# Input order and port use at the start of a macaron block: x ahead of the weights, two rounds of roots, GpSimd scaling eight weight groups

## The reference

```
x = x + 0.5 * ffn(layernorm(x))
x = x + mixer(layernorm(x))          # in-projection, causal conv, state space scan, gate, RMS norm, out-projection
x = x + 0.5 * ffn(layernorm(x))      # the same ffn weights
ffn(v): v = fwht(v * SU_ug) / 64
        u = v @ W_up.T * (Wscale_up * 64);  g = v @ W_gate.T * (Wscale_gate * 64)
        h = fwht(silu(g) * u * SU_dp) / 64
        return h @ W_down.T * (Wscale_dp * 64)
```

## Time and profile before

| what | value |
|---|---|
| time before, median of 3 runs | 1652.19 us (1651.5 to 1653.33) |
| time of the profiled execution | 1654.4 us |
| span of the profiled execution | 1652.4 us |
| PE busy | 1621.7 us, 98% of the span |
| DVE busy | 1034.9 us, 63% |
| ACT busy | 626.4 us, 38% |
| POOL busy | 378.9 us, 23% |

### The profile page before, as it was taken

How to read it: one execution, slowest core, us unless ns; L and a number is a source line. 1 busy time by engine, 2 the same in 40 slices (tenths; PEclk the granted TensorE clock), 3 DMA queues, 4 the chain that set the end, 5 groups by cost and what they waited for, 6 DMA issues and landing times.

```text
span 1652.4 us, 25046 instructions
## 1 busy us (share of the span) xinstructions
PE 1621.7 (98%) x9672; PEld 1312.8 (79%) x9672; DVE 1034.9 (63%) x2022; ACT 626.4 (38%) x934; POOL 378.9 (23%) x298
## 2 busy tenths in 40 slices
PE   6999999989999999999999999999999999999999
PEld 3788888867888778888878888877888878888887
DVE  6444445766676877777786777777675684543333
ACT  4333434454333464333355334256333342122111
POOL 1656663012221212222122122121122121000000
PEclk9999999999999999999999999999999999999999
DMA  9746554745455454444535444445445537556763
GB/s 296 286 151 245 205 217 166 268 156 159 155 159 162 132 177 145 161 161 152 160 121 175 164 150 166 161 138 182 157 154 158 164 117 227 167 181 188 218 201 130
DMA packets 253427, 290.46 MB, mean 176 GB/s; under 512 B 14464, under 2 KB 211200, under 8 KB 244096
## 3 DMA queue, kind: packets, MB, share of 16 engines
q1 hardware_dynamic: 253312, 288.88, 53.4%
HBM read 238.51 MB, written 50.33 MB: 175 GB/s over the span
## 4 chain that ended last, share of the span: by engine, by line
PE 73%; DVE 3%; ACT 2%; issue 1%; DMA 0%; SPq 0%; ACTq 0%; DVEq 0%
PE bank L1185 30%; PE bank L1226 14%; PE bank L1141 12%; PE bank L1254 5%; PE bank L1323 3%; PE bank L1294 2%; PE bank L1310 2%; PE bank L1272 2%; PE bank L1317 1%; PE bank L1282 1%; DVE xT L1741 0%; DVE m_cv L1782 0%; DVE res L1767 0%; DMA cum_stay<-m_aS 0%; PE bank L1169 0%
## 5 line engine op out<-in xcount | busy, mean ns | idle before, releaser
L1185 PE MATMUL bank<-fxT,wj 128*128 128x512 f32 x1752 | 415.3, 390 | 1.3 <-DVE xn L1754 1.3
L1185 PEld LDWEIGHTS bank<-fxT,wj 128*128 128x128 f32 x1752 | 328.6, 188 | 70.2 <-DVE xn L1754 1.7
L1226 PE MATMUL bank<-m_wd,m_hb 128*128 128x512 f32 x1128 | 278.8, 392 | 1.4 <-DVE m_hb L1760 1.4
L1226 PEld LDWEIGHTS bank<-m_wd,m_hb 128*128 128x128 f32 x1128 | 209.1, 188 | 46.5 <-issue 4.1
L1536 ACT CAST m_hb<-xn 128x512 fp32r<-128x512 f32 x96 | 59.5, 620 | 451.8 <-DVE xn L1754 451.8
L1141 PE MATMUL bank<-xT,wi 128*128 128x512 f32 x900 | 223.6, 397 | 1.6 <-DVE m_cv L1782 0.5
L1141 PEld LDWEIGHTS bank<-xT,wi 128*128 128x128 f32 x900 | 166.7, 189 | 39.2 <-issue 4.4
L1767 DVE TENSOR_TENSOR res<-bank,res 128x512 f32<-128x512 f32 x192 | 132.4, 690 | 83.2 <-PE bank L1226 81.1
L2084 POOL TENSOR_TENSOR m_L<-m_L,m_GT 128x512 f32<-128x512 f32 x36 | 52.6, 1462 | 438.0 <-ACT m_L L1545 438.0
L1754 DVE SCALAR_TENSOR_TENSOR xn<-bank,sc,xn 128x512 f32<-128x512 f32 x96 | 71.7, 747 | 120.8 <-PE bank L1185 120.7
L1530 ACT ACTIVATE xn<-bank,sc 128x512 f32<-128x512 f32 x96 | 66.1, 688 | 146.4 <-PE bank L1185 140.9
(11 more groups left out here) (222 smaller groups left out, 2316.2 us busy)
## 6 DMA issues: line engine op xcount, KB each, us to landing
wj<-ug_split SPq DMA_DIRECT2D x167, 512.0 KB, 4.3
m_wd<-dn_split SPq DMA_DIRECT2D x48, 1024.0 KB, 4.8
wi<-in_split SPq DMA_DIRECT2D x76, 512.0 KB, 3.3
ug_split<-b_wu SPq DMA_DIRECT2D x8, 2048.0 KB, 14.0
m_wo<-out_split SPq DMA_DIRECT2D x32, 512.0 KB, 4.1
wi<-ug_split SPq DMA_DIRECT2D x25, 512.0 KB, 4.4
in_split<-b_msp SPq DMA_DIRECT2D x20, 512.0 KB, 3.8
raw<-in_wug SPq DMA_DIRECT2D x8, 1024.0 KB, 6.8
```

Of the source, the lines that this page charges most:

```text
L1185: ins = pe.matmul(to[:], w[:, a, k, :], frm[:, b, k, :], start=(k == 0 and i == 0), stop=(k == KH - 1 and i == 2))
L1226: ins = pe.matmul(F[t % 2][:], hb[:, a, j, ck(t)], wd[:, b, j, :], start=(j == 0 and n == 0), stop=(j == 1 and n == 2))
```

## The change

- SP issues `cs`, `pr` and the last of `cs`, waits until all three have landed (`s_par` 48), then issues groups 0 to 3, `wdp` (with a semaphore of its own, `s_wdp`), the first up chunk, groups 4 to 7, x of sequence 1, groups 8 to 15, and the second up chunk.
- x of sequence 0 and the scales `sc` are issued from ACT's queue, as the first things in its program.
- The third up chunk (`fetch(2)`) is issued ahead of the write of group 15, no longer after that of group 4. The write of the transformed up chunk 0 (`keep_up(0)`, 2 MB) comes after the two reads of `down_half`, no longer after the write of group 8. A wait for it stands ahead of `keep_up(1)`.
- POOL scales groups 0 to 7 instead of 0 to 3, and does not begin before DVE has finished the first round of roots (`s_mv` 1).
- DVE takes statistics and roots for sequence 0 first, then does the butterflies of chunk 0, the low halves of x of sequence 0, those of chunk 0, groups 8 and 9, and then statistics and roots of sequence 1 with groups 10 and 11 between.
- x of sequence 0 is turned before the up chunk 0 on PE and ACT.
- The four turns of x of sequence 1 stand together after `up(0, 2)`, in four banks (`D[0]` to `D[3]`), no longer two after `up(0, 1)` and two after `up(0, 2)` through two banks; ACT writes their rows after group 15.

```diff
-    for key in ([("ug", 0, k) for k in range(KH)] + [("x", 0, t) for t in range(TPG)] + [("x", 1, t) for t in range(TPG)]
+    for key in ([("x", 0, t) for t in range(TPG)] + [("ug", 0, k) for k in range(KH)] + [("x", 1, t) for t in range(TPG)]
...
-            return U[i % 4] if i < 8 else U[key[2]] if key[:2] == ("x", 3) else T[i % 2]
+            return U[i % 4] if i < 8 else D[key[2]] if key[:2] == ("x", 1) else U[key[2]] if key[:2] == ("x", 3) else T[i % 2]
...
             if n == 0:
-                return (), (("x", 1, 0), ("x", 1, 1)), (("x", 1, 2), ("x", 1, 3)), ()
+                return (), (), tuple(("x", 1, t) for t in range(TPG)), ()
...
+            sp.dma_start(cs[:, 0:C_I2], cst[:, 0:C_I2]).then_inc(s_par, 16)
+            sp.dma_start(pr[:], par[:, 0:P_WDP]).then_inc(s_par, 16)
+            sp.dma_start(cs[:, C_I2:C_END], cst[:, 5 * P:5 * P + HEADS]).then_inc(s_par, 16)
+            sp.wait_ge(s_par, 48)
             for i in range(4):
                 load_group(i)
-            sp.dma_start(res[:, 0:TPG, :], xt[:, 0:TPG, :]).then_inc(s_x0, 16)
+            sp.dma_start(wdp[:], par[:, P_WDP:P_END]).then_inc(s_wdp, 16)
+            fetch(0)
+            for i in range(4, 8):
+                load_group(i)
             sp.dma_start(res[:, TPG:2 * TPG, :], xt[:, TPG:2 * TPG, :]).then_inc(s_x1, 16)
-            sp.wait_ge(s_x0, 16)
-            for i in range(4, 12):
+            for i in range(8, FB):
                 load_group(i)
             fetch(1)
...
             for i in range(FB):
+                if i == FB - 1:
+                    fetch(2)
...
                 sp.dma_start(mid_s[:, PQ * i:PQ * (i + 1), :], group_tile(i)).then_inc(s_gs, 16)
-                if i == 4:
-                    fetch(2)
-                if i == 8:
-                    keep_up(0)
             sp.wait_ge(s_gs, 16 * FB)
             fetch_down(0)
             fetch_down(1)
+            keep_up(0)
...
             fetch_down(2)
+            sp.wait_ge(s_us, 16)
             keep_up(1)
...
-            pool.wait_ge(s_par, 64)
-            for i in range(4):
+            pool.wait_ge(s_wdp, 16)
+            pool.wait_ge(s_mv, 1)
+            for i in range(FB // 2):
                 pool.wait_ge(s_gc, i + 1)
                 pool.tensor_tensor(group_tile(i), group_tile(i), wdp[:], ALU.mult).then_inc(s_gp, 1)
-            pool.wait_ge(s_gw, FB // 2)
+            pool.wait_ge(s_gw, FB // 4)
...
             for i in range(4):
                 group(i)
+            for t in range(TPG):
+                turn(("x", 0, t))
+            group(4)
+            group(5)
             for k in range(KH):
                 turn(("ug", 0, k))
-            for i in range(4, 8):
+            for i in range(6, 10):
                 group(i)
...
+            act.dma_start(res[:, 0:TPG, :], x.rearrange("(t p) n -> p t n", p=P)[:, 0:TPG, :]).then_inc(s_x0, 16)
+            act.dma_start(sc[:], wsc.rearrange("c p n -> p c n")).then_inc(s_sc, 16)
+            act.wait_ge(s_par, 48)
...
+            dve.wait_ge(s_x0, 16)
+            for t in range(TPG):
+                own.done(dve.bn_stats(st[:, t, :], res[:, t, :]))
+            run(roots(dve, st[:, 0:TPG], mv[:, :, 0:TPG], own))
+            bias(0, TPG)
             dve.wait_ge(s_fr[0], 16)
             for n, op in enumerate((ALU.add, ALU.subtract)):
                 dve.tensor_tensor(t1[:, n::2, :], raw[:, 0, 0::2, :], raw[:, 0, 1::2, :], op).then_inc(s_b0, 1)
...
+            for t in range(TPG):
+                turn(("x", 0, t))
             for k in range(KH):
                 turn(("ug", 0, k))
-            for t in range(TPG):
-                turn(("x", 0, t))
-            for i in (8, 4, 5, 6, 7, 9):
-                group(i)
+            dve.wait_ge(s_wdp, 16)
+            group(8)
+            group(9)
+            second = stats(TPG, TPG, TPG)
+            dve.wait_ge(s_x1, 16)
+            next(second)
+            next(second)
+            group(10)
+            group(11)
+            next(second)
+            bias(TPG, TPG)
```

More of the change, by code:

```diff
@@ L212, in begin @@
         st, mv = sb("st", [P, 2 * TPG, 6]), sb("mv", [P, 4, 2 * TPG])
-        s_par, s_c, s_ex, s_x0, s_x1, s_x, s_sc = (sem(n) for n in "par c ex x0 x1 x sc".split())
+        s_par, s_wdp, s_c, s_ex, s_x0, s_x1, s_x, s_sc = (sem(n) for n in "par wdp c ex x0 x1 x sc".split())
         s_g, s_gv, s_gc, s_gp, s_gw, s_gs = (sem(n) for n in "g gv gc gp gw gs".split())
@@ L235, in by_vector @@
         def by_vector(i):
-            return i >= 8 and i % 2 == 0
+            return i >= FB // 2 and i % 2 == 0
         def copies(i):
@@ L340, in _ @@
             xt = x.rearrange("(t p) n -> p t n", p=P)
[L341 to L344, removed]
             def load_group(i):
                 sp.dma_start(group_tile(i), wdn[PQ * i:PQ * (i + 1)].rearrange("i (a n) -> a i n", a=FB)).then_inc(s_gl[i], 16)
-            fetch(0)
+            sp.dma_start(cs[:, 0:C_I2], cst[:, 0:C_I2]).then_inc(s_par, 16)
+            sp.dma_start(pr[:], par[:, 0:P_WDP]).then_inc(s_par, 16)
+            sp.dma_start(cs[:, C_I2:C_END], cst[:, 5 * P:5 * P + HEADS]).then_inc(s_par, 16)
+            sp.wait_ge(s_par, 48)
             for i in range(4):
                 load_group(i)
-            sp.dma_start(res[:, 0:TPG, :], xt[:, 0:TPG, :]).then_inc(s_x0, 16)
+            sp.dma_start(wdp[:], par[:, P_WDP:P_END]).then_inc(s_wdp, 16)
+            fetch(0)
+            for i in range(4, 8):
+                load_group(i)
             sp.dma_start(res[:, TPG:2 * TPG, :], xt[:, TPG:2 * TPG, :]).then_inc(s_x1, 16)
-            sp.wait_ge(s_x0, 16)
-            for i in range(4, 12):
+            for i in range(8, FB):
                 load_group(i)
             fetch(1)
-            for i in range(12, FB):
-                load_group(i)
-            sp.dma_start(sc[:], wsc.rearrange("c p n -> p c n")).then_inc(s_sc, 16)
             for i in range(FB):
-                if i < 4:
+                if i == FB - 1:
+                    fetch(2)
+                if i < FB // 2:
                     sp.wait_ge(s_gp, i + 1)
@@ L365, in _ @@
                 else:
-                    sp.wait_ge(s_gw, copies(i) - 3)
+                    sp.wait_ge(s_gw, copies(i) - FB // 2 + 1)
                 sp.dma_start(mid_s[:, PQ * i:PQ * (i + 1), :], group_tile(i)).then_inc(s_gs, 16)
-                if i == 4:
-                    fetch(2)
-                if i == 8:
-                    keep_up(0)
             sp.wait_ge(s_gs, 16 * FB)
@@ L473, in turn @@
                     pe.wait_ge(*((s_sil, 2 * UNITS - 1 + k) if k < 2 else (s_h, 2 * UNITS - 3 + k)))
-                elif i >= 10:
+                elif i >= 12:
                     pe.wait_ge(s_tl, i - 1)
                 elif i >= 8:
-                    group_free(FB - 10 + i)
+                    group_free(FB - 12 + i)
                 elif i >= 4:
@@ L551, in down @@
                     ins.then_inc(s_d, 1)
-            pe.wait_ge(s_par, 64)
+            pe.wait_ge(s_par, 48)
             pe.wait_ge(s_c, 8)
@@ L556, in _ @@
                 group(i)
+            for t in range(TPG):
+                turn(("x", 0, t))
+            group(4)
+            group(5)
             for k in range(KH):
                 turn(("ug", 0, k))
-            for i in range(4, 8):
+            for i in range(6, 10):
                 group(i)
-            for t in range(TPG):
-                turn(("x", 0, t))
-            group(8)
-            group(9)
             for n in range(UNITS):
@@ L607, in rows @@
             def rows(c, ts=range(TPG)):
-                act.wait_ge(s_mv, max(1, c))
+                act.wait_ge(s_mv, c + 1)
                 if c:
@@ L645, in high_half @@
                 act.copy(parts[:, halves[key][1], 0, :], untransformed(key)).then_inc(s_ph, 1)
-            act.wait_ge(s_par, 64)
+            act.dma_start(res[:, 0:TPG, :], x.rearrange("(t p) n -> p t n", p=P)[:, 0:TPG, :]).then_inc(s_x0, 16)
+            act.dma_start(sc[:], wsc.rearrange("c p n -> p c n")).then_inc(s_sc, 16)
+            act.wait_ge(s_par, 48)
             act.activation(s["acol"][:], pr[:, P_ALOG:P_ALOG + 1], ACT.Exp).then_inc(s_ex, 1)
@@ L651, in _ @@
                 group(i)
[L652 to L655, removed]
             rows(0)
@@ L658, in _ @@
                 turn(("x", 0, t))
+            group(4)
+            group(5)
+            for k in range(KH):
+                turn(("ug", 0, k))
             group(6)
@@ L661, in _ @@
             group(9)
-            rows(1)
             act.wait_ge(s_sc, 16)
@@ L680, in _ @@
                     group(15)
+                    rows(1)
                 for key in keys[1]:
@@ L770, in _ @@
             dve.memset(s["ones"][:], 1.0).then_inc(s_c, 1)
-            dve.wait_ge(s_par, 64)
+            dve.wait_ge(s_par, 48)
             dve.tensor_reduce(eight[:], I.rearrange("p (a i) -> p i a", i=PQ), mybir.AxisListType.X, ALU.add).then_inc(s_c, 1)
@@ L810, in _ @@
                 if n == 0:
```

(13 more changed lines are left out.)

## The result

The changed kernel takes 1657.17 us in the median of 6 runs (1655.5 to 1660.06), the kernel before 1652.76 us beside it (6 runs, 1650.75 to 1654.94). The ratio is 1.003, 95% interval 1.0018 to 1.0041: some 4.4 us slower. The forecast was 1651.2 us with a range up to 1654.0 us.

A forecast was written before the change was run, and what follows sets the result against it. PE was taken as the bound, busy 1621.7 of 1652.4 us. `up(0, 0)` 0.6 us later and a 1.6 us stall removed gave -1.0 us, from the 1652.2 us median to 1651.2 us; range 1646.5 to 1654.0 us.

The forecast's parts named there:

- Constants: At the start, the three constants loaded on SP's queue beside x would all have landed at 4.5 us.
- the late bound: Latest landing considered for the constants at the start, behind all of x: 7.0 us.
- rival B: At the start, constants land behind x, holding groups and chunk 0 by 2.5 us: 1653.7 us; chance 0.12.
- the early end: Earliest landing considered for the constants at the start, undisturbed by x: 3.7 us.
- First roots hidden: Before the butterflies, DVE's first roots end at 13.8 us, hidden behind PE's groups and ACT's copies.
- The lock: DVE's chunk 0 butterflies and POOL's scalings block each other and alternate; butterflies end 3.6 us later than alone.
- Rival A: Before `up(0, 0)`, POOL's scaling costs the butterflies little: 1646.8 us; chance 0.2.
- The clock: After idle PE ahead of the up turns, half clock costs 0.8 us, within 0 to 1.7 us.
- Behind `up(0, 0)`: After `up(0, 0)`, second statistics, roots and turns of x cost PE nothing; up to 0.5 us if uncovered.
- The round trip: Groups written to DRAM and read back for `draw` come early enough; PE's stall there goes, -1.6 us.

The follow-up runs named there:

- the middle profile of before: The kernel before, unchanged, profiled a second time: `up(0, 0)` starts at 31.10 us and the first `down` at 65.84 us; own ratio in this set 0.9988.
- both edits together: The changed kernel without SP's wait for the constants and with POOL's scaling held until the four butterflies are done: 1648.97 us, ratio 0.9979 to the kernel before.

## Why the prediction was wrong

It was wrong in sign: -1.0 us against the kernel before was forecast, and +4.4 us came out, 5.4 us apart (6.0 us in the time itself). By its own steps:

- **Constants, taken at 4.5 us: this step failed.** They landed at 7.0 us, the late bound, which is my rival B. The two experiments on it show both halves: issued without x beside them they are used from 3.65 us on, and without SP's wait their lateness leaves no hole in the DMA traffic. I priced B at 2.5 us; the first matmul was 1.75 us later than I took, chunk 0 3.4 us later. I had given B a chance of 0.12 on the argument that the three are small; their size didn't protect them. The first of `cs` landed at 3.7 us, but `pr` and the last of `cs` waited until x was nearly through. The Trainium skill (DMA: Bandwidth & Descriptors, Queues, rings and completion order) says that a DMA engine takes turns between its queues, packet by packet, which I had read as speaking for the early end. The trace bears out no such reading: between 3.5 and 5.0 us SP's queue had no turn at all, and 300 packets of x went by.
- **First roots hidden.** Right: they ended at 14.8 us, rows and turns of x followed at 16.1 to 19.7 us.
- **The lock.** Right in kind, and the size too high: 3.1 us more than alone in one profile, 1.9 us in the other, against 3.6 us worked out. Not every butterfly met a scaling; where all four did (x issued later) it was 4.1 us. Holding POOL back took the whole of it away. Rival A, that it costs little, falls.
- **The clock, taken at 0.8 us.** It costs 1.6 us in one profile and 2.8 us in the other, and the turns behind it are PE's own work. The granted clock fell behind 5.51 and 3.97 us of idle PE, and with x later behind 4.38 us. My 1.7 us for the upper bound was too low.
- **Behind `up(0, 0)`.** Right: second statistics, roots and the four turns together cost PE nothing; it was even 0.3 us less than before.
- **The round trip, -1.6 us: failed as a term of the sum.** The stall went down to 0.28 us as I said, but it was the mark of one execution. The span on which I built, 1652.4 us, was 1.7 us over the median span of 1650.7 us of the kernel's own runs, and two further profiles have no such stall and T 0.5 and 1.0 us earlier.

With the measured values the same sum closes on the middle profile of before: T at 35.5 us against 31.1 us is 4.4 us later, the stall adds 0.3 us and the missing wait of 0.3 us ahead of the turns of x of sequence 1 takes it away; 4.4 us is the measured difference of the medians in the first set, 3.2 us in the second. Of the 5.4 us that the forecast was off, 2.9 us are the butterflies' later end (chunk 0 3.4 us later, the lock 0.5 us less than taken), 0.4 us the clock, 1.9 us the stall, and 0.5 us the early T of that profile, less 0.3 us for the missing wait.

Small rows alone don't make the constants late: with the same rows they landed 1.8 to 2.5 us after their issue, both without x beside them and ahead of x on one queue. What stays open is by what rule x's packets go first. It isn't simply the order of issue: in the version without SP's wait `sc`, 16 KB in small packets, was issued by ACT at 1.2 us, ahead of the groups of SP's queue, but moved beside them once x had landed and took 10.4 us to landing. No run here varied the size of the packets.

## What to carry to other kernels

A wait on a small load ahead of a chain of large ones is dear if something large is issued beside the small load, and holding the large one back instead gave only 1.0 us here; so leave the wait out and let each engine wait for what it reads. Work moved to GpSimd cost VectorE 1.9 to 4.1 us over four instructions that read two operands from SBUF, so place it behind VectorE's critical instructions, not merely behind an earlier milestone: that one line took the lock away whole, and both edits together turned 0.2 to 0.3% slower into 0.2% faster. And before a stall of one or two us is booked as a gain, look for it in a second profile of the same kernel.

## What the runs showed of the hardware

The spread of this kernel's times goes largely with the clock. Of the 93 runs of the kernel before that stand beside the experiments, the 28 with a mean granted clock of 0.996 have a median span of 1651.6 us, the 28 with 0.999 one of 1648.5 us. In the profiles looked at, the falls sit at two places: before 31 us, and where the mixer begins, where PE idles again. From the first profile of before and from that after, busy time by stretch:

```profile
360.00:365.00 5.00, 2.80 (x20) 1.90 (x18) 3.42 (x7) 4.05 (x7) 0.00 (x0) 0.99 0.63 223
365.00:370.00 5.00, 4.31 (x14) 2.97 (x13) 2.15 (x4) 2.15 (x4) 0.00 (x0) 0.67 0.00 0
```

```profile
360.00:365.00 5.00, 4.32 (x54) 3.02 (x52) 2.79 (x4) 2.59 (x5) 0.00 (x0) 1.00 0.42 111
365.00:370.00 5.00, 2.79 (x11) 2.00 (x12) 3.75 (x7) 2.69 (x5) 0.00 (x0) 1.00 0.35 141
```

The kernel before fell there in its profiled execution and the changed one did not, which is part of why the two spans, 1652.4 and 1653.7 us, lie only 1.3 us apart while the medians lie 4.4 us apart: from F to the end it is 1584.4 and 1583.5 us. The larger part is that F itself was 2.2 us later in that first profile of before than in the middle one. Whether the clock falls at such a place differs from run to run of one kernel: of three profiles of before it fell in two, and in the version without SP's wait the runs at a mean clock of 1.0 have a median span of 1648.0 us, those at 0.996 to 0.997 some 5 us more. A single profile shows where an idle stretch is, and not what it costs in the median.
